# A cross-attention and feed-forward layer on Trainium2: the weight units of up and down are turned by VectorE's block transposes, and up takes one scale for all its rows

## The reference

```python
x = x + xattn(layernorm(x), ctx, ...)        # 16 heads of 32, rope, causal, softmax, output projection
h = act_qdq(layernorm(x))                    # int16 steps of one scale for the whole tensor
up   = act_qdq(h @ lpbq_dequant(w_up).T)     # w_up [1536, 512]
gate = act_qdq(h @ lpbq_dequant(w_gate).T)
gate = act_qdq(gate * fixed_qdq_u16(sigmoid(gate)))
o    = act_qdq(gate * up)
x = x + o @ lpbq_dequant(w_down).T           # w_down [512, 1536]

def lpbq_dequant(w):                         # 4 bits, blocks of 32 along the inner dimension
    wb = w.reshape(O, I // 32, 32)
    s = max(max(abs(wb), axis=-1) / 7, 1e-12)
    return (clip(round(wb / s), -8, 7) * s).reshape(O, I)
```

## Time and profile before

| | us |
|---|---|
| median of 3 runs (lowest to highest) | 1556.7 (1555.59 to 1557.77) |
| the profiled execution: its run | 1558.91 |
| the profiled execution: its span | 1557.1 |

### The profile page before, as it was taken

How to read it: one execution, slowest core, us unless ns; L and a number is a source line. 1 busy time by engine, 2 the same in 40 slices (tenths; PEclk the granted TensorE clock), 3 DMA queues, 4 the chain that set the end, 5 groups by cost and what they waited for, 6 DMA issues and landing times.

```text
span 1557.1 us, 24459 instructions
## 1 busy us (share of the span) xinstructions
PE 1385.5 (89%) x9294; PEld 787.1 (51%) x9294; DVE 1189.2 (76%) x1793; ACT 946.4 (61%) x2016; POOL 341.1 (22%) x326
## 2 busy tenths in 40 slices
PE   4799999999999999869999998999999005999999
PEld 3566676667676676534444444444444002444444
DVE  5878888888888888647777775888899799556541
ACT  7778888888888888743222223999644795212210
POOL 1354455555555544410111110000000000000000
PEclk9999999999999999979999999999999557999999
DMA  6111121111121212112333332766656986445532
GB/s 226 52 56 56 62 69 69 69 69 68 66 82 61 70 63 62 46 41 75 115 122 109 122 116 101 251 243 248 217 179 208 379 301 203 163 137 189 190 120 81
DMA packets 81732, 200.56 MB, mean 129 GB/s; under 512 B 7760, under 2 KB 7760, under 8 KB 78672
## 3 DMA queue, kind: packets, MB, share of 16 engines
q1 hardware_dynamic: 81616, 199.00, 36.5%
HBM read 128.72 MB, written 70.25 MB: 128 GB/s over the span
## 4 chain that ended last, share of the span: by engine, by line
PE 48%; issue 5%; DVE 1%; DMA 1%; ACT 0%; SPq 0%; POOLq 0%; POOL 0%
PE ffn_banks L1118 31%; PE ffn_banks L1136 16%; PE ffn_banks L1094 1%; DMA ffn_ring<-sigs_dram 1%; DVE ffn_wide L1284 0%; DVE ffn_rises L1289 0%; DVE ffn_peaks L1291 0%; DVE ffn_wide L1283 0%; ACT ffn_rest L1176 0%; ACT ffn_ring L1167 0%; DVE ffn_wide L1420 0%; DVE qg L1382 0%; ACT qg L1176 0%; PE ffn_banks L1124 0%; DVE ffn_wide L1433 0%
## 5 line engine op out<-in xcount | busy, mean ns | idle before, releaser
L1118 PE MATMUL ffn_banks<-ffn_wide,ffn_rest 128*128 128x512 f16 x2304 | 504.6, 380 | 10.4 <-DVE ffn_wide L1284 6.1
L1118 PEld LDWEIGHTS ffn_banks<-ffn_wide,ffn_rest 128*128 128x128 f16 x2304 | 225.8, 98 | 279.7 <-issue 15.1
L1136 PE MATMUL ffn_banks<-ffn_rest,ffn_wide 128*128 128x512 f16 x1152 | 251.0, 381 | 96.4 <-DVE ffn_wide L1427 96.4
L1136 PEld LDWEIGHTS ffn_banks<-ffn_rest,ffn_wide 128*128 128x128 f16 x1152 | 113.2, 98 | 234.2 <-issue 99.8
L609 ACT ACTIVATE qg<-score_banks,neg_max 128x128 f32<-128x128 f32 (+1 forms) x512 | 208.4, 454 | 19.3 <-DVE neg_max L499 19.3
L1176 ACT ACTIVATE ffn_rest<-ffn_banks,ffn_row_back 128x1024 f32<-128x1024 f32 x72 | 79.7, 1107 | 156.3 <-PE ffn_banks L1118 146.9
L1255 ACT ACTIVATE ffn_u_steps<-ffn_ring,ffn_scales 128x1024 int16<-128x1024 f32 x48 | 55.0, 1148 | 158.9 <-DMA ffn_ring<-ups_dram 121.0
L423 POOL TENSOR_TENSOR qg<-qg,per_sum 128x512 f32<-128x512 f32 x64 | 82.8, 1293 | 272.8 <-DVE per_sum L503 272.8
L425 POOL TENSOR_TENSOR qg<-qg,per_sum 128x1024 f32<-128x1024 f32 x64 | 134.6, 2103 | 0.0
L609 ACT ACTIVATION_READ_ACCUMULATOR qg<-score_banks,neg_max 128x1 f32 x512 | 122.7, 240 | 0.0
L616 ACT ACTIVATE pt<-ring_banks 128x512 f32<-128x512 f32 x128 | 70.7, 614 | 43.4 <-PE ring_banks L738 42.5
(11 more groups left out here) (176 smaller groups left out, 2685.7 us busy)
## 6 DMA issues: line engine op xcount, KB each, us to landing
ups_dram<-ffn_rest SPq DMA_DIRECT2D x48, 512.0 KB, 3.0
ffn_ring<-ups_dram SPq DMA_DIRECT2D x48, 512.0 KB, 4.2
ffn_wide<-ups_dram SPq DMA_DIRECT2D x17, 1024.0 KB, 8.0
gates_dram<-ffn_rest SPq DMA_DIRECT2D x24, 512.0 KB, 2.6
ffn_ring<-gates_dram SPq DMA_DIRECT2D x24, 512.0 KB, 4.6
ffn_rest<-w_parts_dram SPq DMA_DIRECT2D x36, 256.0 KB, 3.8
x_in<-in_x SPq DMA_DIRECT2D x16, 512.0 KB, 3.7
qg<-in_ctxt SPq DMA_DIRECT2D x16, 512.0 KB, 5.6
```

The costliest lines, as they stand in the source:

```text
L1118: last = pe.matmul(banks[:, pair_of(s), half, :], w[:, m % 2, wp, c, :], xq[:, xp, n, c, :], start=(k == 0), stop=(k == 3 * DC - 1))
L1136: last = pe.matmul(down_banks[:, g % 2, t, :], oq[:, g % 2, op, m, t * P:(t + 1) * P], w_down[:, wp, wk, c], start=(start and k == 0), sto ...
```

## The change

Up's and down's units are no longer turned by TensorE. One VectorE instruction, `dve.transpose`, transposes each 32x32 block of the 128x512 unit in place of its block and writes to the same PSUM bank, one slot earlier in the order (`unit_at` + 1 in place of after piece `unit_at` + 2). That the result is the whole transpose, the host lays the units out so that the blocks stand in each other's places (`by_blocks`). A partition then holds blocks of four different rows, so up can no longer have a scale per row: it takes one power of two for all, `up_inv`, from six more sums in attention. The scans run as 12 from iteration 3 on, the first six for up, the last six for down at iterations 9 to 14 as before; a join MX 11 for up stands at iteration 9, that for down stays at 15. Three small operations fall out of `quantise` for up. The gate's units stay as they are.

```diff
-DOWN_SCAN, DOWN_SCANS = 9, 6
-JOINS = ((0, 3), (3, 2)) + tuple((5 + n, 1) for n in range(9))
+DOWN_SCAN, DOWN_SCANS = 3, 12
+JOINS = ((0, 3), (3, 2)) + tuple((5 + n, 1) for n in range(10))
...
 PE_AFTER = {(i, "S", 3): [("MX", 2 + k, 0)] for i, k in LATE_SETS}
+PE_AFTER[DOWN_SCAN + DOWN_SCANS // 2, "S", 2] = [("MX", 11, 0)]
 PE_AFTER[DOWN_SCAN + DOWN_SCANS, "S", 2] = [("MX", 10, 0)]
...
+DVE_AFTER[DOWN_SCAN + DOWN_SCANS // 2, "max", 2] = [("scale", 11, 0)]
...
             if col == D_COL:
-                return [8 + BATCH + k for k in range(DOWN_SCANS)]
+                return [8 + BATCH + k for k in range(DOWN_SCANS // 2, DOWN_SCANS)]
+            if col == U_COL:
+                return [8 + BATCH + k for k in range(DOWN_SCANS // 2)]
...
-                sp.dma_start(down_in[:, :].rearrange("p (u d) -> p u d", d=D), down_scans[2 * IC // 2 + k]).then_inc(down_loaded, 16)
+                sp.dma_start(down_in[:, :].rearrange("p (u d) -> p u d", d=D), down_scans[IC // 2 + k]).then_inc(down_loaded, 16)
...
-                    elif lo == D_COL:
-                        dve.tensor_copy(keep["down_inv"][:, :], inv[:, D_COL:D_COL + 1]).then_inc(scaled, 1)
-                        dve.tensor_copy(keep["down_half"][:, :], half[:, D_COL:D_COL + 1]).then_inc(dve_step, 1)
+                    elif lo in (D_COL, U_COL):
+                        which = "down" if lo == D_COL else "up"
+                        dve.tensor_copy(keep[which + "_inv"][:, :], inv[:, lo:lo + 1]).then_inc(scaled, 1)
+                        dve.tensor_copy(keep[which + "_half"][:, :], half[:, lo:lo + 1]).then_inc(dve_step, 1)
...
-            def turn_unit(u):
-                pe.wait_ge(w_dequantised, u + 1)
-                if u >= 2:
-                    pe.wait_ge(w_split, u - 1)
-                for c in range(DC):
-                    last = pe.transpose(banks[:, 3, u % 2, c * P:(c + 1) * P], w_deq[:, u % 2, c * P:(c + 1) * P],
-                                        keep["ident"][:, :])
-                last.then_inc(w_turned, 1)
...
-                for u in range(2 * IC):
-                    if unit_at[u] + 2 == s:
-                        turn_unit(u)
...
-                if u < IC:
-                    power = keep["row_power"][:, IC + u:IC + u + 1]
-                    link(dve.tensor_reduce(row_step[:, :], st, AX.X, ALU.max))
-                    link(dve.tensor_scalar(power.bitcast(I32), row_step[:, :].bitcast(I32), EXPONENT, None, ALU.bitwise_and))
-                    link(dve.tensor_scalar(row_inv[:, :].bitcast(I32), power.bitcast(I32), EXPONENT, None, ALU.bitwise_xor))
...
-                link(dve.tensor_scalar(st, st, row_inv[:, :] if u < IC else keep["down_inv"][:, :], None, ALU.mult))
+                link(dve.tensor_scalar(st, st, keep["up_inv" if u < IC else "down_inv"][:, :], None, ALU.mult))
...
+            def turn_unit(u):
+                dve.wait_ge(w_dequantised, u + 1)
+                if u >= 2:
+                    dve.wait_ge(w_split, u - 1)
+                dve.transpose(banks[:, 3, u % 2, :], w_deq[:, u % 2, :]).then_inc(w_turned, 1)
...
                     if unit_at[u] + 3 == s:
                         split_unit(u)
+                    if unit_at[u] + 1 == s:
+                        turn_unit(u)
                     if unit_at[u] == s:
                         quantise(u)
-            dve.tensor_scalar(row_back[:, IC:2 * IC], keep["row_power"][:, IC:2 * IC], sc["x_step"], 0.5, ALU.mult,
+            dve.tensor_scalar(row_back[:, IC:2 * IC], keep["ones"][:, 0:IC], sc["x_step"], keep["up_half"][:, :], ALU.mult,
                               ALU.mult).then_inc(u_backed, 1)
...
+    by_blocks = lambda w: w.reshape(IC, 4, 32, DC, 4, 32).transpose(0, 4, 2, 3, 1, 5).reshape(IC, P, D)
```

More of the change, by code:

```diff
@@ L235, in attend @@
         bv_scaled = buf("bv_scaled", [P, DC], F32)
[L236 to L239, removed]
+        top = buf("top", [P, 15], F32)
+        power = buf("power", [P, 15], F32)
+        inv = buf("inv", [P, 15], F32)
+        half = buf("half", [P, 15], F32)
         row_step = buf("row_step", [P, 1], F32)
@@ L246, in attend @@
         ident = keep["ident"]
-        Q_COL, K_COL, V_COL, O_COL, D_COL = 0, 1, 3, 4, 13
+        Q_COL, K_COL, V_COL, O_COL, D_COL, U_COL = 0, 1, 3, 4, 13, 14
         def c_set(i):
@@ L844, in feed_forward @@
         per_step = buf("per_step", [P, D // QBLOCK], F32)
-        row_step = buf("row_step", [P, 1], F32)
-        row_inv = buf("row_inv", [P, 1], F32)
         qg = keep["qg"]
@@ L1458, in build @@
             "ones": ctx.enter_context(nc.sbuf_tensor("ones", [P, P], F32)),
-            "row_power": ctx.enter_context(nc.sbuf_tensor("row_power", [P, 2 * IC], F32)),
+            "row_power": ctx.enter_context(nc.sbuf_tensor("row_power", [P, IC], F32)),
+            "up_inv": ctx.enter_context(nc.sbuf_tensor("up_inv", [P, 1], F32)),
+            "up_half": ctx.enter_context(nc.sbuf_tensor("up_half", [P, 1], F32)),
             "down_inv": ctx.enter_context(nc.sbuf_tensor("down_inv", [P, 1], F32)),
@@ L1485 @@
         "attn_wt": np.stack([np.asarray(w).T for w in (L0_xattn_Wq, L0_xattn_Wk, L0_xattn_Wv, L0_xattn_Wo)]),
-        "ffn_w": np.concatenate([units(L0_ffn_w_gate), units(L0_ffn_w_up),
-                                 np.asarray(L0_ffn_w_down).reshape(DC, P, INNER // D, D).transpose(0, 2, 1, 3)
-                                 .reshape(IC, P, D)]),
+        "ffn_w": np.concatenate([units(L0_ffn_w_gate), by_blocks(units(L0_ffn_w_up)),
+                                 by_blocks(np.asarray(L0_ffn_w_down).reshape(DC, P, INNER // D, D).transpose(0, 2, 1, 3)
+                                           .reshape(IC, P, D))]),
         "bqk": np.concatenate([np.asarray(L0_xattn_bq).reshape(DC, P), np.asarray(L0_xattn_bk).reshape(DC, P)]).T,
```

## The result

| | before | after |
|---|---|---|
| median, us (lowest to highest) | 1557.8 (1555.59 to 1563.48), 20 runs | 1555.07 (1551.03 to 1561.09), 20 runs |
| ratio, 95% interval | | 0.9977 [0.9967, 0.9988] |
| profiled execution: run, span | 1558.91, 1557.1 | 1558.21, 1556.4 |

By this ratio the change is worth 3.6 us (1.9 to 5.1), half of the 7.3 predicted; the two medians are 2.7 us apart. The median lies just above the range given. The runs of both kernels spread by 8 to 10 us, and their mean granted clock spreads with them: of the 26 runs of the kernel before that ran beside `turn_only`, 15 had a clock of 0.957 to 0.959 and took 1555.1 to 1558.0 us, 11 had 0.954 or 0.955 and took 1560.2 to 1564.2.

A forecast was written before the change was run, and what follows sets the result against it. TensorE was taken to bound the first pass and, less tightly, attention. Terms -10.5 + 1.6 (sums) + 1.6 (join) = -7.3 us, from a median of 1556.7 to 1549.4 us; range 1545.8 to 1555.0.

The forecast's parts named there:

- Transposes off TensorE: First pass of the feed-forward block: 24 units at 0.44 us each leave TensorE's path, 10.5 us less.
- the reading of the evacuations: First pass: pieces evacuate 5.18 us apart without a unit between, 5.62 with one, so 0.44 us a unit.
- The price on VectorE: First pass: one 128x512 f32 block transpose takes 0.73 us, like the 32-partition shuffle; 0.75 with issue.
- the prediction's other estimates for a unit: First pass, VectorE: 1.24 us from the skill's 311 ns per 128x128 bf16, or 2.5 us doubled for f32.
- VectorE's occupied time: First pass: VectorE, with up's removed operations and 24 added transposes, occupied 202.2 of 233.2 us, 87%.
- The rival in which VectorE becomes the bound: First pass: a transpose over 2.04 us makes VectorE the bound; 1570.0 us at 2.9 us each; chance 0.06.
- Six sums: Attention iterations 3 to 8: odd ones cost 0.50 us each, even ones 0.03, together 1.6 us more.
- The join: Attention iteration 9: six sums as twelve small TensorE instructions delay the next matmul, 1.6 us more.
- VectorE's six small operations come while it would wait for O; 0: Attention iteration 9: the join's operations on VectorE, 0.15 to 0.17 us each, fill waiting time and cost 0.
- The clock: Rival: half clock follows iteration 9's join, or lasts longer at the second-pass handoff; 2 us more, 1551.4; chance 0.15.

The follow-up runs named there:

- turn_only: Changed kernel with attention as in the kernel before and up's units scaled by down's power of two; 1550.63 us, ratio 0.9949.
- join_only: Kernel before plus a join at iteration 9 of six sums it has anyway, result not used; 1563.03 us, ratio 1.0029.
- six_ops: Kernel before plus six 128x1 memsets on VectorE at iteration 9, without a join on TensorE; 1563.70 us, ratio 1.0018.
- after_again: Changed kernel measured once more without any edit; 1554.03 us, ratio 0.9960 to the kernel before.
- op_behind: Changed kernel plus one small memset at the end of VectorE's attention program; 1554.26 us, ratio 0.9958 to the kernel before.
- one_more_op: Changed kernel plus one small memset at the start of VectorE's attention program; 1554.44 us, ratio 0.9949 to the kernel before.
- one_join: Changed kernel without the join at iteration 9; at 15 one matmul and one reduction serve up and down; 1549.32 us, ratio 0.9947.
- lean_join: Changed kernel with each join as one six-column matmul plus one more small VectorE operation; 1552.13 us, ratio 0.9954 to the kernel before.

## Why the prediction was wrong, point by point

- **Transposes off TensorE, -10.5:** 10.48 in every kernel with the change. Right, and so was the reading of the evacuations.
- **The price on VectorE, 0.73 us from the shuffle:** 0.716. Right, and both of the prediction's other estimates for a unit, 1.24 and 2.5 us, were too long. VectorE's occupied time came to 233.27 - 35.7 = 197.6 us, where I had 202.2: a turn adds 0.56 us (197.6 - 184.2, over 24), since records overlap at their ends by some 0.1 us. The rival in which VectorE becomes the bound had a wide margin against it.
- **Six sums, +1.6:** 1.0 to 1.6 in the profiles, 3.1 (0.8 to 5.3) timed. Right within what can be told.
- **The join, +1.6:** its stretch is longer by 40.67 - 39.45 = 1.2, and without the accident the next is shorter by 39.14 - 38.67 = 0.5, so 0.7 for itself. Over-sized: the 1.64 us of the earlier trace rows lie in part at the lower clock (645.00 to 646.00 us has a granted clock of 0.53), while at iteration 9 of `join_only` the next matmul starts 1.26 us behind the join's first. And part of it is had back from idle time in the stretch behind.
- **"VectorE's six small operations come while it would wait for O; 0":** this is the step that failed. They do hide where they stand (39.42 us for the join's stretch in `six_ops`, 39.39 before), but they move every later instruction of VectorE's program by some places, and in iteration 10 one instruction came 0.26 us late, behind GpSimd in a race that it wins in every other iteration: 1.9 us. The prediction had no term for two engines that hold each other up.
- **The clock:** it was a rival with 0.15 and 2 us in all. In the profile of after there are two such stretches at iterations 9 and 10, 1.7 us or so each, and the one of iteration 15 is longer, for another 1.7. The one right behind the join, which the rival names, is in two of the eight profiles with a join at iteration 9.

With the runs' terms: -10.5 + 1.6 + 0.7 + 1.9 = -6.3 us, to compare with -6.2 (`after_again`) and -6.5 (`op_behind`); without the accident -8.2, to compare with -7.9 (`one_more_op`).

The 0.9977 of the first set is 2.7 us less gain, which is more than its interval allows, and more than the net 1.0 us by which these terms correct the sum. The agreement with the later sets is in part luck: the changed kernel's medians hardly differ (1555.07, 1554.03), but the kernel before had 1557.8 us in the first set and 1561.99 and 1560.82 beside `after_again` and `op_behind`. So the larger part of the miss is open.

More half clock could fill it. The mean clock of the changed kernel's first 20 runs is 0.9550, and that of the 26 runs before beside `turn_only`, with a median of 1557.5, is 0.9566, where one stretch of 3.4 us lowers it by 0.0011 (3.4 x 0.5 / 1557); in the set of `after_again` the two are 0.9557 and 0.9554. By that the first set would have one or two such stretches more, 1.7 to 3.4 us. But the clocks of its own runs before are not on record, and where the stretches fell in its 19 unprofiled runs is not seen, so that part is argued and not shown.

The baseline adds to the miss in the time: the median of before over 20 runs is 1.1 us above that of the three runs that I had. Three runs did not show that some take 1560 to 1564 us, and a range of 9 us around one number was too sure for a kernel that spreads so.

## What to carry to other kernels

Price an added instruction not only by its time: where the end of one operation releases another engine while its own engine goes on at once, and the two can hold each other up, ask who is first and by how much, and read the margin in the rows (here GpSimd started 0.28 us behind the reciprocal and VectorE 0.12 behind it). A stretch that got longer without being touched by the change is best tested by shifting the program with an operation that does nothing, with the same operation behind the place as control. A sum over few columns can go in one matmul and one reduction instead of twelve small matmuls, and at a place where a join stands anyway: `one_join` has 0.9947, the lowest ratio of the kernels here that compute all of the reference, though the intervals of `lean_join` and `one_more_op` overlap it. And when the ratio of the same kernel differs between sets, look at the two medians: here it was the kernel before that moved.

## What the runs showed of the hardware

- VectorE's block transpose of 128x512 f32 from SBUF to PSUM takes 0.716 us, as a shuffle does (0.728), and GpSimd's scaling and ScalarE's evacuations in that stretch are not slower (1.05 and 1.11 us, as before).
- One VectorE instruction, the 621st of the profile, was issued 0.26 us late in six executions; with another number of instructions before it, the same instruction was not late in eight. Why that place is slow is open; no run here looks behind "issue". In all six a transfer of 8 KB on the queue q14, of the kind "instruction", starts 0.67 to 0.95 us behind the start of the late one, which points to the loading of code and does not show it.
- In a clash of VectorE with GpSimd here the first to start keeps its time. Where that is GpSimd, VectorE's operations end 0.03 and 0.28 us behind GpSimd's: 0.97 us in place of 0.12, and 2.07 in place of 0.43. Where it is VectorE, GpSimd's take 1.32 us in place of 1.04 and 2.34 in place of 1.89. A 128x16 operation can thus cost 0.85 us more.
- A wait of TensorE of 2.1 us was followed within 1 us by a half-clock stretch in four of six executions, and one such stretch costs some 1.7 us (39.57 against 37.91). It moves between runs of the same kernel.
